# Self attention stage: copying the repeated high parts of the score stacks on the chip instead of loading them twice

## Chip, cores and metric

One NeuronCore of a Trainium2 chip runs the whole kernel. The metric is the device time of the program in microseconds (us). The profile is one execution of the same program, with times of instructions and transfers.

## What is computed

A gated block of two attentions over x, 32 batches of 100 rows and 512 columns, 16 heads of 32:

```
x = x + tanh(g_xattn) * cross_attention(layernorm(x), ctx_1024)
x = x + tanh(g_ffn)   * self_attention(layernorm(x))
```

The change touches the second line alone. There queries, keys and values come from one product, a similarity of each query with a guide vector sorts the 95 token rows of a batch into two classes, each class attends to its own class and to 5 register rows, and the register rows get the mean of what they would get with either class:

```
q, k, v = split(layernorm(x) @ W_qkv);  sim = mean over heads of cos(q, q_g), scaled to 0..1;  pos = sim > 0.9
logits  = (q * HD**-0.5) @ k^T                       # per batch and head, 100 x 100
x_pos, x_neg = softmax(logits | keys of pos) @ v, softmax(logits | keys of not pos) @ v
reg_out = (x_pos[:REG] + x_neg[:REG]) / 2;  tok_out = where(pos, x_pos, x_neg)
out     = concat(reg_out, tok_out) @ W_proj + b_proj
```

## The kernel before, in words

Four stages follow each other: `stage_queries`, `stage_cross`, `stage_rows` (projections of the second attention, written to DRAM as `qk_parts`, `values`, `x1` and the class `tables`) and `stage_self` (L1563), which is the last 340 us and the only one whose loops change.

**Split operands.** fp32 products are made from parts: a high part rounded to the fp32r type and the low rest. `qk_parts` holds four of them: q high, q low, k high, k low, each 512 x 3200. A score product is q_hi k_hi + q_lo k_hi + q_hi k_lo. The kernel gets it from one matmul per head by stacking along the contraction: `q_stack` has the 32 dims of q high in partitions 0 to 31, of q low in 32 to 63, of q high again in 64 to 95; `k_stack` has k high in 0 to 31, k high again in 32 to 63, k low in 64 to 95. Partitions 96 and 97 of both hold two class rows (the tables), which mask the keys. One stack holds a pair of batches (2 x 100 columns) for 16 heads. There are STACKS = 3 buffers of each, so pair n uses buffer n % 3. Pair 0 is loaded in `stage_rows`.

**Loads of a pair** (`load_pair` in the SyncE block; `load_stacks` L928, DMAs L932; `load_tables` L936, DMAs L941 and L943). Eight DMAs: q high and low together, q high again, k high again, k high and low together (two of 800 KB and two of 400 KB), and four small ones for the tables. All count on `pair_in[buf]`.

**Register copies** (`copy_registers` L947, done at L951 by GpSimd): the five register queries are put a second time into the q stack, for the second class. They read partitions 0 to 95, so they wait for the pair. For pair n they stand in batch 2n - 2.

**A batch.** Every engine's program is written out by hand as `body(b)`, six in a row for the buffers and a loop over them (`all_batches`); the bodies are software pipelined: body(b) scores batch b + 1, turns and mixes batch b, and projects batch b - 1. In body(b):

- TensorE: turn_probs(b, 0), score(b+1, 0), turn 1, score 1, turn 2, score 2, mix(b, 0) and (b, 1), half of project(b-1), turn 3, score 3, the other half, mix(b, 2) and (b, 3). Lines: turn L1834, score L1827, mix L1845, project L89 to L91.
- ScalarE: high_part(b-1) (L1705), then exponentials(b+1, 0 to 3), each four ACTIVATEs of one head (L1713).
- VectorE: turn_back(b, 0), shift_of(b+1, 0), fold_registers(b-1) (L1762, L1764), turn_back 1, split_mix(b-1) (L1768), shift 1, turn_back 2, shift 2, invert(b+1, 0), turn_back 3, shift 3, invert 1, result(b-1), invert 2, invert 3. Lines: turn_back L1750, shift_of L1739, invert L1746, result L1775. result(b-1) writes `y[odd]`, so it waits until the store of two batches before has left that buffer (`stored`).
- GpSimd: scale(b+1, j) (L1679) behind each invert, which frees turn_probs(b+1, j).
- SyncE's DMA queue, one for all of this stage's transfers, in order: store(b-1) (L1635, waits for result(b-1)), the x1 rows of batch b + 2 (L1619), the values of batch b + 3 (L1616, waits for the end of mix(b, 3)), and in an even body the eight loads of pair b/2 + 3 (wait for the last score of pair b/2). A DMA that waits holds all behind it.

So pair n + 3 is asked for in body(2n) and first needed by the register copies of body(2n + 4).

Of the kernel before, what the change touches and what calls it, by code (L numbers as in the profile page):

```python
# [23 lines left out]
ACT = mybir.ActivationFunctionType  # L24
# [45 lines left out]
def f32(ap):  # L70

    return ap.bitcast(F32)
# [814 lines left out]
STACKS = 3  # L887
# [6 lines left out]

QUERIES_AT = S
TW = QUERIES_AT + S + 2 * SIDE
A_PAIR_LOADS = 8


PLACED = 2  # L900
# [24 lines left out]
        self.cleared, self.copies_done = m.sem("cleared"), m.sem("copies_done")  # L925


def load_stacks(engine, qk_parts, q_stack, k_stack, first, landed):  # L928
# [634 lines left out]
def stage_self(nc, shared, begin, qk_parts, values_dram, x1_dram, table_dram, out):  # L1563
    with ExitStack() as ctx:
# [26 lines left out]
        proj_full, y_ready = m.sem("proj_full"), m.sem("y_ready")  # L1591
        stored = [m.sem(f"stored{i}") for i in range(2)]
        cleared = m.sem("cleared")

        block = ctx.enter_context(nc.Block())

        def all_batches(engine, body):


            for i in range(RING):  # L1600
                body(i, i, i // DEEP, i // 2, i, False)
            with engine.Fori(1, TAIL // RING) as u:
                for i in range(RING):
                    body(u * RING + i, i, u * (RING // DEEP) + i // DEEP, u * STACKS + i // 2, RING, False)
            for b in range(TAIL, B):
                body(b, b % RING, b // DEEP, b // 2, RING, b == B - 1)

        @block.sync
        def _(sp):
            def load_pair(first, buf):  # L1610

                load_stacks(sp, qk_parts, q_stack[buf], k_stack[buf], first, pair_in[buf])
# [10 lines left out]
            load_pair(2, 1)  # L1623
            load_values(1, 1)
            load_x1(0, 0)
            load_x1(1, 1)
            for n in range(2, DEEP):
                load_values(n, n)
                load_x1(n, n)
            for n in range(2, STACKS):  # L1630
                load_pair(2 * n, n)
# [24 lines left out]
            for b in range(TAIL, B):  # L1656
                body(b, b % RING, b // DEEP, b // 2, RING, b == B - 1, b + DEEP - 1 < B, b + DEEP < B, b + RING < B)
            store(B - 1, 1)
            for odd in range(2):
                sp.wait_ge(stored[odd], 16 * B // 2)  # L1660

        @block.gpsimd
        def _(pool):
            gaps = [(buf, at) for buf in range(1, STACKS) for at in (REG, 2 * QR - 1)]
            for n, (buf, at) in enumerate(gaps):
                if n:
                    pool.wait_ge(cleared, n)
# [3 lines left out]
            def copies(buf, pairs_before):  # L1671
                pool.wait_ge(pair_in[buf], (pairs_before + 1) * 16 * A_PAIR_LOADS)
                copy_registers(pool, q_stack[buf], unit_column, copies_done)

            def scale(b, odd, j):

                pool.wait_ge(inv_done, b * HPT + j + 1)
                quarter = prob[:, j, :, :]
                pool.tensor_tensor(quarter, quarter,  # L1679
                                   repeated(inv[odd][:, j * KT:(j + 1) * KT].unsqueeze(2), 2, S), ALU.mult  # L1680
                                   ).then_inc(scaled, 1)

            for b in range(RING):
                for j in range(HPT):
                    scale(b, b % 2, j)
                if b % 2 == 0:
                    copies((b + 2) // 2 % STACKS, (b + 2) // RING)
            with pool.Fori(1, TAIL // RING) as u:
                for i in range(RING):
                    for j in range(HPT):  # L1690
                        scale(u * RING + i, i % 2, j)
                    if i % 2 == 0:
                        copies((i + 2) // 2 % STACKS, u + (i + 2) // RING)
            for b in range(TAIL, B):
                for j in range(HPT):
                    scale(b, b % 2, j)
                if b % 2 == 0 and b + 2 < B:
                    copies((b + 2) // 2 % STACKS, (b + 2) // RING)

        @block.scalar  # L1700
        def _(act):
# [15 lines left out]
            def body(b, i, deep, pair, before, last):  # L1717
                odd = i % 2
                if before:
                    high_part(b - 1, 1 - odd)  # L1720
                if not last:
# [12 lines left out]
        def _(dve):  # L1734
# [43 lines left out]
            def body(b, i, deep, pair, before, last):  # L1778
                odd = i % 2
                turn_back(b, 0)  # L1780
                if not last:
                    shift_of(b + 1, 0)
# [33 lines left out]

        @block.tensor
        def _(pe):
            def score(b, i, j, pairs_before):

                buf, odd = i // 2, i % 2
                if not odd and j == 0:
                    pe.wait_ge(pair_in[buf], (pairs_before + 1) * 16 * A_PAIR_LOADS)
# [36 lines left out]
            def body(b, i, deep, before, last, step):  # L1860
# [2 lines left out]
                    pe.wait_ge(pt_done, b * HPT - 1)  # L1863
                turn_probs(b, 0)
                if not last:
                    score(b + 1, at, 0, step + (i + 1) // RING)
                if before:
                    pe.wait_ge(pt_done, b * HPT)
                turn_probs(b, 1)
# [20 lines left out]
                mix(b, odd, 3, place, deep)  # L1890

            for j in range(HPT):
                score(0, 0, j, 0)
# [56 lines left out]
```

## Time and profile before

| | us |
|---|---|
| device time, median of 3 runs | 2592.28 |
| lowest and highest | 2587.09, 2594.41 |
| the profiled execution: its own device time | 2588.93 |
| the profiled execution: span of the profile | 2587.1 |
| busy in the span: TensorE matmul, VectorE, ScalarE, GpSimd | 2478.7, 1804.8, 1332.2, 491.6 |

The page of the profile gives busy time for whole engines, the span in 40 slices of 64.7 us, and the costliest groups of instructions. The self stage is slices 35 to 40. A row of a timeline gives start, duration, engine, line, output <- input, and in brackets the idle time of the engine just before with what ended it.

### The profile page before, as it was taken

How to read it: one execution, taken by the hardware profiler on the slowest of the kernel's cores; microseconds unless marked ns; L12 is line 12 of the kernel's file. 1: busy time of each engine (PE TensorE's matmuls, PEld its weight loads, DVE VectorE, ACT ScalarE, POOL GpSimd, SP SyncE). 2: the span in 40 equal slices, each digit the busy share in tenths (PEclk: the TensorE clock that was granted, in tenths of full speed). 3: DMA queues.
4: the chain of work that ended last, by engine and by line, in shares of the span. 5: the costliest groups of instructions: out<-in, count | busy, mean ns of one | idle time of the engine just before them, and what ended most of it. 6: DMA issues, size and time to landing. Idle time of an engine off the chain costs nothing. (4 is left out here: it accounts for less than half of the span.)

```text
span 2587.1 us, 47522 instructions
## 1 busy us (share of the span) xinstructions
PE 2478.7 (96%) x17128; PEld 2223.4 (86%) x17128; DVE 1804.8 (70%) x2998; ACT 1332.2 (51%) x3000; POOL 491.6 (19%) x412
## 2 busy tenths in 40 slices
PE   6899999999999999999999999999959999889998
PEld 6889999999999999999999999999858888677776
DVE  7567777777777777777777777777757666565665
ACT  3355555555555545555555555545534444455564
POOL 0311111111111111111111111111024333133333
PEclk9999999999999999999999999999969999889999
DMA  7645554555545555545554455554459999899994
GB/s 223 205 122 131 124 131 120 131 128 131 132 117 128 130 133 128 131 117 130 129 132 122 128 125 129 131 132 126 106 150 192 214 211 198 207 175 189 192 185 105
DMA packets 324312, 379.82 MB, mean 147 GB/s; under 512 B 125814, under 2 KB 231702, under 8 KB 324118
## 3 DMA queue, kind: packets, MB, share of 16 engines
q1 hardware_dynamic: 322414, 375.71, 61.2%
q8 instruction: 132, 2.16, 0.4%
q10 hardware_dynamic: 1704, 1.43, 0.2%
q14 instruction: 62, 0.51, 0.1%
HBM read 162.48 MB, written 72.57 MB: 91 GB/s over the span
## 5 line engine op out<-in xcount | busy, mean ns | idle before, releaser
L740 DVE TENSOR_TENSOR c_parted<-c_prob,c_parted 128x600 fp32r<-128x600 f32 x512 | 400.6, 783 | 363.4 <-ACT c_prob L686 363.4
L864 PE MATMUL c_mix<-c_parted,c_v 120*66 120x200 f32 (+1 forms) x3072 | 544.9, 270 | 0.7 <-DVE c_parted L740 0.6
L849 PEld LDWEIGHTS c_pair<-c_q_stack,c_k_stack 100*120 100x120 f32 (+1 forms) x3072 | 517.7, 186 | 10.7 <-issue 6.1
L849 PE MATMUL c_pair<-c_q_stack,c_k_stack 100*120 100x100 f32 (+1 forms) x3072 | 520.0, 227 | 6.1 <-DVE c_parted L740 4.5
L726 DVE TENSOR_REDUCE c_peak<-c_pair 100x1 f32<-100x724 f32 x512 | 456.9, 908 | 55.2 <-PE c_pair L811 39.7
L682 ACT ACTIVATE c_parted<-c_pair 128x600 fp32r<-128x600 f32 x512 | 344.9, 674 | 283.0 <-PE c_pair L849 282.8
L864 PEld LDWEIGHTS c_mix<-c_parted,c_v 120*66 120x66 f32 (+1 forms) x3072 | 418.3, 140 | 3.1 <-DVE c_parted L740 0.9
L664 ACT ACTIVATE c_v<-c_work 120x512 fp32r<-120x512 f32 (+1 forms) x192 | 115.7, 603 | 442.3 <-PE c_work L91 442.3
L686 ACT ACTIVATE c_prob<-c_pair 128x600 f32<-128x600 f32 x512 | 341.4, 667 | 0.0
L811 PE MATMUL c_pair<-c_k_stack,c_q_stack 96*100 96x362 f32 x1024 | 254.4, 329 | 0.0
L617 POOL TENSOR_TENSOR c_ct_lo<-e_stage,c_ct_hi 128x722 fp32r<-128x722 f32 x64 | 111.8, 1747 | 747.1 <-ACT c_ct_hi L650 747.1
L617 POOL TENSOR_TENSOR f_ct_lo<-e_stage,f_ct_hi 128x722 fp32r<-128x722 f32 x60 | 104.8, 1747 | 718.5 <-ACT f_ct_hi L650 718.5
L811 PEld LDWEIGHTS c_pair<-c_k_stack,c_q_stack 96*100 96x100 f32 x1024 | 169.6, 166 | 60.4
L674 ACT ACTIVATE c_k_hi<-c_work,f_key_bias 128x362 fp32r<-128x362 f32 (+1 forms) x256 | 144.9, 567 | 105.3 <-PE c_work L91 85.7
L720 DVE SCALAR_TENSOR_TENSOR c_k_lo<-c_work,f_key_bias,c_k_hi 128x362 fp32r<-128x362 f32 (+1 forms) x256 | 149.8, 586 | 54.4 <-ACT c_k_hi L674 54.4
L1713 ACT ACTIVATE s_prob<-s_scores,s_shift 106x100 f32<-106x100 f32 x512 | 168.1, 368 | 34.5 <-DVE s_shift L1739 34.5
L89 PE MATMUL c_work<-f_ct_hi,w_wk_hi 128*128 128x362 f32 (+1 forms) x512 | 176.7, 345 | 8.6 <-PEq L153 4.5
L89 PE MATMUL c_work<-c_ct_hi,w_wk_hi 128*128 128x362 f32 (+1 forms) x512 | 175.0, 342 | 0.0
L91 PE MATMUL c_work<-f_ct_hi,w_wk_lo 128*128 128x362 f32 (+1 forms) x512 | 169.4, 331 | 0.0
L90 PE MATMUL c_work<-f_ct_lo,w_wk_hi 128*128 128x362 f32 (+1 forms) x512 | 169.1, 330 | 0.0
L91 PE MATMUL c_work<-c_ct_hi,w_wk_lo 128*128 128x362 f32 (+1 forms) x512 | 167.9, 328 | 0.0
L90 PE MATMUL c_work<-c_ct_lo,w_wk_hi 128*128 128x362 f32 (+1 forms) x512 | 167.9, 328 | 0.0
(205 smaller groups left out, 5292.7 us busy)
## 6 DMA issues: line engine op xcount, KB each, us to landing
c_k_stack<-c_k_hi SPq DMA_DIRECT2D x1024, 90.2 KB, 2.1
e_stage<-in_ctx SPq DMA_DIRECT2D x32, 1444.0 KB, 6.3
c_k_stack<-c_k_lo SPq DMA_DIRECT2D x512, 90.2 KB, 2.1
c_q_stack<-q_parts SPq DMA_DIRECT2D x192, 100.0 KB, 2.4
mix_parts<-w_mixed SPq DMA_DIRECT2D x64, 200.0 KB, 3.2
r_parts<-mix_parts SPq DMA_DIRECT2D x22, 512.0 KB, 7.1
s_q_stack<-qk_parts SPq DMA_DIRECT2D x10, 800.0 KB
s_k_stack<-qk_parts SPq DMA_DIRECT2D x10, 800.0 KB
```

Source lines behind the costliest of these rows:

```text
L89: pe.matmul(out, left_hi, right_hi, start=first, stop=False)
L90: pe.matmul(out, left_hi, right_lo, start=False, stop=False)
L91: return pe.matmul(out, left_lo, right_hi, start=False, stop=last)
L617: pool.tensor_tensor(ct_lo[odd][:, k, :], columns[:, k, :], ct_hi[odd][:, k, :], ALU.subtract).then_inc(ct_lo_done, 1)
L682: act.activation(parted[i % PR][:, :, 0, :].rearrange("p (a t) s -> p a t s", a=2), logits, ACT.Exp).then_inc(exp_hi_done, 1)
L686: act.activation(prob[i % 2][:, :, :].rearrange("p (a t) s -> p a t s", a=2), logits, ACT.Exp).then_inc(exp_done, 1)
L726: dve.tensor_reduce(peak[:, i:i + 1], pair[i % 2][0:S, :, 0:HALF], AX.XY, ALU.max).then_inc(peak_done, 1)
L740: dve.tensor_tensor(p[:, :, 1, :], prob[i % 2][:], p[:, :, 0, :], ALU.subtract).then_inc(p_lo_done, 1)
L811: last = pe.matmul(pair[i % 2][0:S, bank, 0:HALF], q_stack[0:STACK, i, :], k_stack[0:STACK, i, cols], start=True, stop=True)
L849: return pe.matmul(pair[i % 2][0:r, t // (CT // 2), col:col + S], k_stack[:, i, c_cols(t)], q_stack[:, i, :], start=True, stop=True)
L864: return pe.matmul(mix[g % 2][0:VW, at * 2 * S:(at + 1) * 2 * S], v[0:r, t, i, :], parted[i % PR][0:r, t, :, :].rearrange("p a s -> p (a s)"),
L1713: last = act.activation(prob[:, j, k, :], scores[0:QR, j, k * S:(k + 1) * S], ACT.Exp, bias=shift[:, at:at + 1], scale=-1.0, accum_out=tot ...
```

## The change

From pair 3 on `load_pair` issues only the first of each stack's two loads: q high and low into partitions 0 to 63, and k high and low into 32 to 95. The other third of each stack is copied on the chip in four pieces of four heads, 32 partitions by 4 x 200 columns: the q third by ScalarE (partitions 0 to 31 to 64 to 95), the k third by VectorE (partitions 32 to 63 to 0 to 31). Both do the pieces of pair b/2 + 2 in body(b): pieces 0 and 1 in the even body, 2 and 3 in the odd one, one after the first half of the exponentials (ScalarE) or ahead of turn_back 3 (VectorE), one at the end of the exponentials or ahead of result. Each piece waits for all of the pair's loads. GpSimd's register copies and the pair's first score now wait for the pieces too. Pairs 0 to 2 are loaded whole as before; the order of the two k loads is exchanged in all pairs. Bodies 2 to 27 hold the pieces of pairs 3 to 15.

```
+WHOLE_LOADS, PAIR_LOADS = 8, 6
+def pair_landed(buf, before):
+    return 16 * (PAIR_LOADS * (before + 1) + (WHOLE_LOADS - PAIR_LOADS if buf < WHOLE_PAIRS else 0))
...
-    for stack, at, places in ((q_stack, SIDE, ((0, 0, 2), (2, 0, 1))), (k_stack, 0, ((0, 2, 1), (1, 2, 2)))):
-        for place, part, parts in places:
+    for stack, at, places in ((q_stack, SIDE, ((0, 0, 2), (2, 0, 1))), (k_stack, 0, ((1, 2, 2), (0, 2, 1)))):
+        for place, part, parts in places if whole else places[:1]:
...
+        def thirds_in(i, before, more):
+            ahead = (i + 4 - i % 2) // 2
+            if not more or (before < RING and ahead < WHOLE_PAIRS):
+                return 0, 0, ()
+            return ahead % STACKS, ahead // STACKS, (2, 3) if i % 2 else (0, 1)
...
# GpSimd, ahead of copy_registers
+                if whole is not True:
+                    pool.wait_ge(q_third, HPT * (STACKS * pairs_before + buf - WHOLE_PAIRS + 1))
...
# ScalarE
+            def copy_third(buf, before, n):
+                act.wait_ge(pair_in[buf], pair_landed(buf, before))
+                heads = slice(n * HPT, (n + 1) * HPT)
+                act.activation(q_stack[buf][2 * HD:3 * HD, heads, SIDE:SIDE + 2 * S],
+                               f32(q_stack[buf][0:HD, heads, SIDE:SIDE + 2 * S]), ACT.Copy).then_inc(q_third, 1)
...
                 if not last:
-                    for j in range(HPT):
-                        exponentials(b + 1, 1 - odd, j)
+                    exponentials(b + 1, 1 - odd, 0)
+                    exponentials(b + 1, 1 - odd, 1)
+                for n in pieces[:half]:
+                    copy_third(buf, u + turns, n)
+                if not last:
+                    exponentials(b + 1, 1 - odd, 2)
+                    exponentials(b + 1, 1 - odd, 3)
+                for n in pieces[half:]:
+                    copy_third(buf, u + turns, n)
...
# VectorE
+            def copy_third(buf, before, n):
+                dve.wait_ge(pair_in[buf], pair_landed(buf, before))
+                heads = slice(n * HPT, (n + 1) * HPT)
+                dve.tensor_copy(k_stack[buf][0:HD, heads, 0:2 * S], f32(k_stack[buf][HD:2 * HD, heads, 0:2 * S])
+                                ).then_inc(k_third, 1)
...
                     invert(b + 1, 1 - odd, 0)
+                for n in pieces[:half]:
+                    copy_third(buf, u + turns, n)
                 turn_back(b, 3)
                 if not last:
                     shift_of(b + 1, 3)
                     invert(b + 1, 1 - odd, 1)
+                for n in pieces[half:]:
+                    copy_third(buf, u + turns, n)
...
# TensorE, ahead of the first score of a pair
+                    if not whole:
+                        pe.wait_ge(q_third, HPT * (STACKS * pairs_before + buf - WHOLE_PAIRS + 1))
+                        pe.wait_ge(k_third, HPT * (STACKS * pairs_before + buf - WHOLE_PAIRS + 1))
```

## Rows read from the trace of the kernel before

**Rows 1.** The page: busy share of the 16 DMA engines in 40 slices.
```profile
DMA  7645554555545555545554455554459999899994
```

**Rows 2.** Starts of mix(b, 2) and (b, 3) on TensorE, b = 4, 28, 30.
```profile
2315.31 1.31 PE L1845 MATMUL s_out_bank<-s_pt,s_values 100*32 100x106 f32 x16
...
2551.43 1.31 PE L1845 MATMUL s_out_bank<-s_pt,s_values 100*32 100x106 f32 x16
...
2568.31 1.31 PE L1845 MATMUL s_out_bank<-s_pt,s_values 100*32 100x106 f32 x16
```

**Rows 3.** Waits, self stage (engine, line, releaser: us in total, times, longest).
```profile
DVE s_y L1775 <- DMA out<-s_y: 39.9, 13, 5.7
```

**Rows 4.** SyncE's queue, pair 7's loads in body 8 (start, duration).
```profile
2362.47 2.76 SPq L932 DMA_DIRECT2D s_q_stack<-qk_parts  x2
...
2378.03 1.23 SPq L943 DMA_DIRECT2D s_q_stack<-tables  x1
2379.35 0.67 SPq L1635 DMA_DIRECT2D out<-s_y  x1
```

**Rows 5.** DMA issues by line and size: the large load of a stack.
```profile
s_q_stack<-qk_parts SPq DMA_DIRECT2D x10, 800.0 KB
```

**Rows 6.** Stretches: us, busy (x count) of PE, PEld, DVE, ACT, POOL, PEclk, DMA share, GB/s.
```profile
2286.00:2298.00 12.00, 12.00 (x109) 9.87 (x108) 9.07 (x25) 8.99 (x51) 4.31 (x7) 1.00 1.12 203
2298.00:2302.00 4.00, 4.00 (x39) 3.18 (x37) 1.17 (x3) 2.68 (x16) 1.30 (x2) 1.00 0.37 91
...
2326.00:2338.00 12.00, 11.85 (x111) 9.89 (x109) 9.31 (x25) 8.02 (x45) 5.46 (x8) 1.00 1.13 182
...
2542.00:2562.00 20.00, 19.63 (x181) 16.02 (x180) 13.28 (x36) 13.02 (x74) 9.27 (x13) 1.00 0.34 114
```

**Rows 7.** Timeline of an undisturbed batch: body 10 and the start of body 11.
```profile
2365.22 0.57 PE L1834 MATMUL s_turned<-e_ident,s_prob 106*100 106x106 f32 x4
...
2369.74 0.17 DVE L1746 RECIPROCAL s_inv<-s_total 106x4 f32<-106x4 f32 x1
2370.76 0.60 DVE L1750 COPY s_pt<-s_turned 100x424 f32<-100x424 f32 x1 [0.85 <-PE s_turned L1834]
...
2372.72 0.75 DVE L1775 SCALAR_TENSOR_TENSOR s_y<-s_out_bank,p_gate,s_x 100x512 f32<-100x512 f32 x1 [0.79 <-PE s_out_bank L91]
...
2373.63 1.67 POOL L1679 TENSOR_TENSOR s_prob<-s_prob,s_inv 106x400 f32<-106x400 f32 x2 [0.78 <-DVE s_inv L1746]
...
2375.11 0.55 PE L1834 MATMUL s_turned<-e_ident,s_prob 106*100 106x106 f32 x4
```

**Rows 8.** Groups by form: mean ns of one stands after the busy us.
```profile
L726 DVE TENSOR_REDUCE c_peak<-c_pair 100x1 f32<-100x724 f32 x512 | 456.9, 908 | 55.2 <-PE c_pair L811 39.7
...
L1440 DVE COPY w_mixed<-w_mixed 32x224 f32<-32x224 f32 x1 | 0.3, 265 | 0.0
...
L650 ACT ACTIVATE c_ct_hi<-e_stage 128x722 fp32r<-128x722 f32 x64 | 51.0, 796 | 0.0
```

**Rows 9.** Timeline near 2267 us: GpSimd beside a VectorE instruction with two inputs.
```profile
2267.07 0.59 POOL L951 TENSOR_TENSOR s_q_stack<-s_q_stack,p_unit_column 96x80 fp32r<-96x80 f32 x2 [8.18 <-DMA s_q_stack<-tables]
2267.63 3.29 POOL L1679 TENSOR_TENSOR s_prob<-s_prob,s_inv 106x400 f32<-106x400 f32 x4
2267.73 5.33 DVE L1806 TENSOR_TENSOR s_w_lo<-e_stage,s_w_hi 128x2048 fp32r<-128x2048 f32 x1 [1.62 <-ACT s_w_hi L1726]
```

**Rows 10.** A group by form: the same operation and shape in the stage before.
```profile
L1304 DVE TENSOR_TENSOR r_w_lo<-r_raw,r_w_hi 128x2048 fp32r<-128x2048 f32 x1 | 2.3, 2282 | 0.0
```

**Rows 11.** SyncE's queue: first loads of pairs 1 and 3, last table of pair 3.
```profile
2249.64 1.29 SPq L932 DMA_DIRECT2D s_q_stack<-qk_parts  x2
...
2284.54 3.01 SPq L932 DMA_DIRECT2D p_q_stack<-qk_parts  x2
...
2298.33 1.36 SPq L943 DMA_DIRECT2D p_q_stack<-tables  x1
```

**Rows 12.** VectorE's wait for a store in body 3.
```profile
2305.20 0.75 DVE L1775 SCALAR_TENSOR_TENSOR s_y<-s_out_bank,p_gate,s_x 100x512 f32<-100x512 f32 x1 [5.69 <-DMA out<-s_y]
```

More of the change, by code:

```diff
@@ L925, in __init__, with load_stacks @@
         self.cleared, self.copies_done = m.sem("cleared"), m.sem("copies_done")
-def load_stacks(engine, qk_parts, q_stack, k_stack, first, landed):
-    for stack, at, places in ((q_stack, SIDE, ((0, 0, 2), (2, 0, 1))), (k_stack, 0, ((0, 2, 1), (1, 2, 2)))):
-        for place, part, parts in places:
+def load_stacks(engine, qk_parts, q_stack, k_stack, first, landed, whole=True):
+    for stack, at, places in ((q_stack, SIDE, ((0, 0, 2), (2, 0, 1))), (k_stack, 0, ((1, 2, 2), (0, 2, 1)))):
+        for place, part, parts in places if whole else places[:1]:
             src = qk_parts[part:part + parts].rearrange("a (d h) n -> (a d) h n", h=H)
@@ L1600, in all_batches, with load_pair @@
             for i in range(RING):
-                body(i, i, i // DEEP, i // 2, i, False)
+                body(i, i, i // DEEP, i // 2, i, False, 0)
             with engine.Fori(1, TAIL // RING) as u:
                 for i in range(RING):
-                    body(u * RING + i, i, u * (RING // DEEP) + i // DEEP, u * STACKS + i // 2, RING, False)
+                    body(u * RING + i, i, u * (RING // DEEP) + i // DEEP, u * STACKS + i // 2, RING, False, u)
             for b in range(TAIL, B):
-                body(b, b % RING, b // DEEP, b // 2, RING, b == B - 1)
+                body(b, b % RING, b // DEEP, b // 2, RING, b == B - 1, b // RING, (b + 4 - b % 2) // 2 < PAIRS)
+        def thirds_in(i, before, more):
[3 more added lines that the diff above has]
+            return ahead % STACKS, ahead // STACKS, (2, 3) if i % 2 else (0, 1)
         @block.sync
         def _(sp):
-            def load_pair(first, buf):
-                load_stacks(sp, qk_parts, q_stack[buf], k_stack[buf], first, pair_in[buf])
+            def load_pair(first, buf, whole=False):
+                load_stacks(sp, qk_parts, q_stack[buf], k_stack[buf], first, pair_in[buf], whole)
                 load_tables(sp, table_dram, q_stack[buf], k_stack[buf], first, pair_in[buf])
@@ L1622, in _ @@
             sp.wait_ge(cleared, 2 * (STACKS - 1))
-            load_pair(2, 1)
+            load_pair(2, 1, True)
             load_values(1, 1)
@@ L1630, in _ @@
             for n in range(2, STACKS):
-                load_pair(2 * n, n)
+                load_pair(2 * n, n, True)
             def store(b, odd):
@@ L1669, in _, with copies @@
             pool.wait_ge(cleared, 2 * (STACKS - 1))
-            def copies(buf, pairs_before):
-                pool.wait_ge(pair_in[buf], (pairs_before + 1) * 16 * A_PAIR_LOADS)
+            def copies(buf, pairs_before, whole=False):
+                pool.wait_ge(pair_in[buf], pair_landed(buf, pairs_before))
+                if whole is not True:
+                    pool.wait_ge(q_third, HPT * (STACKS * pairs_before + buf - WHOLE_PAIRS + 1))
                 copy_registers(pool, q_stack[buf], unit_column, copies_done)
@@ L1686, in _ @@
                 if b % 2 == 0:
-                    copies((b + 2) // 2 % STACKS, (b + 2) // RING)
+                    copies((b + 2) // 2 % STACKS, (b + 2) // RING, (b + 2) // 2 < WHOLE_PAIRS)
             with pool.Fori(1, TAIL // RING) as u:
@@ L1697, in _ @@
                 if b % 2 == 0 and b + 2 < B:
-                    copies((b + 2) // 2 % STACKS, (b + 2) // RING)
+                    copies((b + 2) // 2 % STACKS, (b + 2) // RING, (b + 2) // 2 < WHOLE_PAIRS)
         @block.scalar
@@ L1715, in exponentials, with body @@
                 last.then_inc(exp_done, 1)
-            def body(b, i, deep, pair, before, last):
+            def copy_third(buf, before, n):
[3 more added lines that the diff above has]
+                               f32(q_stack[buf][0:HD, heads, SIDE:SIDE + 2 * S]), ACT.Copy).then_inc(q_third, 1)
+            def body(b, i, deep, pair, before, last, u, more=True):
                 odd = i % 2
@@ L1720, in body @@
                     high_part(b - 1, 1 - odd)
+                buf, turns, pieces = thirds_in(i, before, more)
+                half = len(pieces) // 2
                 if not last:
-                    for j in range(HPT):
-                        exponentials(b + 1, 1 - odd, j)
+                    exponentials(b + 1, 1 - odd, 0)
[7 more added lines that the diff above has]
+                    copy_third(buf, u + turns, n)
                 if not before:
@@ L1776, in result, with body @@
                                          ).then_inc(y_ready, 1)
-            def body(b, i, deep, pair, before, last):
+            def copy_third(buf, before, n):
[3 more added lines that the diff above has]
+                                ).then_inc(k_third, 1)
+            def body(b, i, deep, pair, before, last, u, more=True):
                 odd = i % 2
+                buf, turns, pieces = thirds_in(i, before, more)
+                half = len(pieces) // 2
                 turn_back(b, 0)
@@ L1818, in _, with score @@
         def _(pe):
-            def score(b, i, j, pairs_before):
+            def score(b, i, j, pairs_before, whole=False):
                 buf, odd = i // 2, i % 2
                 if not odd and j == 0:
-                    pe.wait_ge(pair_in[buf], (pairs_before + 1) * 16 * A_PAIR_LOADS)
+                    pe.wait_ge(pair_in[buf], pair_landed(buf, pairs_before))
                     pe.wait_ge(copies_done, 2 * STACKS * pairs_before + 2 * buf + 2)
+                    if not whole:
+                        pe.wait_ge(q_third, HPT * (STACKS * pairs_before + buf - WHOLE_PAIRS + 1))
+                        pe.wait_ge(k_third, HPT * (STACKS * pairs_before + buf - WHOLE_PAIRS + 1))
                 for k in range(KT):
@@ L1865, in body @@
                 if not last:
-                    score(b + 1, at, 0, step + (i + 1) // RING)
+                    score(b + 1, at, 0, step + (i + 1) // RING, before < RING and (i + 1) // 2 < WHOLE_PAIRS)
                 if before:
@@ L1892, in _ @@
             for j in range(HPT):
-                score(0, 0, j, 0)
+                score(0, 0, j, 0, True)
             for i in range(RING):
```

3 lines of the change are left out of this document (2 added, 1 removed).

## The prediction

> **What bounds the kernel now.** I read the page first. The last six slices, the self stage, show DMA busy at eight or nine tenths, where the long cross stage shows four or five [rows 1]. A share says little alone, so I then took the pace. The start of mix(b, 2), (b, 3) marks each batch: from b = 4 to 28 it takes 2551.43 - 2315.31 = 236.1 us, 9.84 us a batch or **19.68 a pair**; from b = 28 to 30, with no pair left to load, (2568.31 - 2551.43) / 2 = 8.44 a batch or **16.88 a pair** [rows 2]. TensorE is busy 19.63 of 20 us there, at clock 1.00, with DMA at 0.34 [rows 6]. So 2.8 us in each pair is not computation. The list of waits says what it is: result waits 39.9 us in 13 times for `out`, the store two batches before [rows 3]. The store is small, but SyncE's queue shows what it stands behind: pair 7's loads take from 2362.47 to 2379.26 to issue, and only then the next store goes [rows 4]. Issuing is slow since the DMA engines are full: 1.12 and 1.13 busy while the stacks are loaded [rows 6]. The chain is: bytes, queue, store, result, the inverts behind result on VectorE, GpSimd's scale, TensorE's turn. The self stage is bound by its transfers.
>
> **What the change removes.** A pair has 2 x (800 + 400) KB of stack loads [rows 5], 1200 KB of values, x1 and out, and some 50 KB of tables: 3.65 MB. Two of 400 KB go: 2.85 MB. At the present pace bytes alone would allow 19.68 x 2.85 / 3.65 = 15.4 us a pair, below the 16.88 of computation. So the bytes stop being the bound, and the most that 12 pairs, from b = 4 to 28, can give is 12 x 2.80 = 33.6 us.
>
> Stretches of the trace show that the engines are not evenly loaded: 1.12 while stacks are loaded, 0.37 in the 4 us behind pair 3's loads [rows 6]. The Trainium skill (DMA: Bandwidth & Descriptors, Why a DMA increments its semaphore by 16 and not by 1) says that a transfer uses as many engines, up to 16, as divide its slowest dimension: 16 for the stacks, 10 for rows of 100, 2 for the tables. By that rule, my estimate is that the busiest engine goes from 296 to 246 KB a pair, and the bound by transfers would be 16.4 instead of 15.4 us. Both are below 16.88, so the sum is the same.
>
> **What it adds on VectorE.** One copy of 32 x 800 in each place. The nearest rows: a COPY of 224 elements takes 265 ns, a reduction of 724 takes 908 ns [rows 8]. In proportion these give 0.95 and 1.00 us; if half of the small copy's time were a fixed part, 0.13 + 0.47 = 0.60. I take 0.65, since the copy is the same operation and a part of so short a time will be fixed; ends 0.55 and 1.0. The gaps: after invert 0 VectorE is idle 0.85 us until turn_back 3, and 0.79 before result [rows 7]. At 0.65 both copies fit into them; at 1.0 each pushes by 0.2. Behind result stand invert 2 and 3; scale 2 starts at 2373.63, lasts 0.84, and its turn starts at 2375.11 [rows 7], so 0.6 us is spare. Cost: nothing, cover 0.6 us.
>
> **What it adds on ScalarE.** An ACTIVATE of 722 elements between SBUF tiles takes 796 ns [rows 8], so 0.88 us for 800, twice a batch. The first delays exponentials 2 and 3 by about 0.7. Exponential 2 was done near 2371.7, its invert stands behind result until 2373.4, and invert 3 would slip from 2373.5 to 2373.9, whose turn comes 4 us later. The second stands in ScalarE's wait for the fold. Cost: nothing.
>
> GpSimd's register copies and the first score wait for pieces made a body or more before: nothing.
>
> **The new wait.** This is the term that decides. Pair n + 3 was needed in body(2n + 4); its first pieces now stand in body(2n + 2), a pair earlier, and VectorE and ScalarE stand still until all of it has landed. Count from the first turn of an even body: in body 10 that is 2365.22, invert 0 ends at 2369.91, so the piece is due at +4.7; result ends at +8.25 [rows 7]. Store, x1 and values go then, and the loads follow 1.5 us later. About 1.0 us of lateness is absorbed (the 0.6 us above, and the gaps that the copies leave).
>
> How long do loads take to land? Pair 3's started at 2284.54 on quiet engines, its last table went at 2299.69 [rows 11]; the engines were full from 2286 to 2298, then at 0.37 [rows 6]. That is 1.5 to start, 12.3 for the stacks, about 3 for the tail. For two thirds of the stacks: 1.5 + 8.2 + 3 = 12.7. In steady state 600 KB of store, x1 and values stand directly ahead; at 203 GB/s [rows 6] they add 3. From the store's issue at +8.3 that is 15.7 minus the overlap of the start, **15 to 15.7**, so landing at +23.3 to +24.0. The next piece is due one pair later at P + 4.7 + 1.0. So P = 17.6 to 18.3: the loop through the landing, not the computation, sets the pace. Bounds: pair 1, issued at 2249.64 and landed at 2267.07 [rows 9, 11], took 17.4 for a whole pair with other loads beside it; two thirds are 11.6, which gives P = 16.88 (computation bounds). If nothing were gained over its 17.4, P = 17.4 + 9.8 - 5.7 = 21.5. I take **P = 18.0**: 12 x (19.68 - 18.0) = 20.2 us gained.
>
> **The start.** Pair 3's loads are issued at 2284.54 as before, since SyncE is still busy with whole pairs 1 and 2. Its pieces stand in body 2, which begins at about 2284.4, so they are due at 2289.1; it lands at 2284.5 + 12.7 = 2297.2. Wait 8.1, of which 1.0 is absorbed, and about 1 us comes back as TensorE's lower clock behind the stall: 8 us. In exchange, the wait of 5.69 us for store 0 in body 3 [rows 12], which cost 6.9 with its clock, is gone, since the store's queue is shorter. Net loss 1.2 us.
>
> **Sum.** The profiled execution took 2588.9 us (span 2587.1). 2588.9 - 20.2 + 1.2 = **2570 us**, 0.7% less. The profiled execution lies 3.4 us under the median of 2592.3, a difference that the range covers.
>
> **Rivals.**
> *Full gain.* The loads land in 12 to 13 us, P = 16.9: 2588.9 - 33.6 + 1.2 = 2556. For it: two thirds of pair 1's time. Against: store, x1 and values right ahead of each load. Chance 0.2.
> *VectorE's copies collide with GpSimd.* The trace shows VectorE's L1806 taking 5.33 us while four scales ran beside its first 3.19 [rows 9], where the same operation took 2.28 [rows 10]: it stood until GpSimd was done. If a copy behaves so, one behind invert 0 meets the scale which that invert frees. If VectorE comes first, a scale with 1.5 us or more to spare is late, and nothing is lost. If GpSimd does, both copies wait 0.85 us, and result is late by about 1.2, of which 0.6 is lost. On top of P = 18.0 half of it shows: 24 batches x 0.3 = 7, so 2577. Chance 0.15.
> The Trainium skill (SBUF — State Buffer, SBUF: two separate sides) states that the two engines share a port pair as an exclusive lock, taken by VectorE instructions in a two-port mode or with two SBUF inputs; the trace agrees for the two-input kind with the 5.33 us, and no row before shows a copy beside GpSimd.
> *The expected gain is eaten.* Landing takes 17 us from the store's issue, P = 19.6: 2588.9 + 1.2 - 1 = 2589, within 0.3%. Chance 0.13.
> *Slower: the earlier deadline.* The pieces' deadline is a pair earlier, so three stacks work as two: the next loads go only behind a result which stands behind the pieces, and the engines run dry in each loop. It decides from P = 19.8, a landing 17.2 us after the store's issue. At the upper bound P = 21.5: 2588.9 + 1.2 + 12 x 1.8 = 2612. For it: 0.37 busy behind pair 3, a slow tail that does not shrink with the bytes [rows 6]. Against: no third of the bytes has ever been without weight on full engines. Chance 0.1.
>
> **Numbers.** Forecast 0.42; full gain 0.2; collision 0.15; eaten 0.13; slower 0.1. The predicted time is the forecast's. The range goes from the full gain, 2556, up to 2588, which leaves out the slower case and most of the eaten one. About 0.3% (8 us) is what a measurement of this kernel can tell from none. Faster by more: 0.77; within: 0.13; slower: 0.1.
>
> **What would show it.** Result's wait for `out` falls from 39.9 us to under 5. New waits for `tables` appear before the copies in VectorE and ScalarE: 8 us in body 2, 0 to 2 us in each even body. Mix marks stand 17.3 to 18.8 us a pair from b = 4 to 28. 26 bodies x 2 copies of about 0.65 us on VectorE and 0.88 on ScalarE. DMA moves 10.6 MB less. Wrong if the marks stay at 19.7, or if copies wait for GpSimd each time.

## The result, and the profile after

The changed kernel takes **2584.3 us** in the median of 16 runs (2579.96 to 2586.95), the kernel before 2592.22 us in 16 runs beside them (2585.11 to 2596.53). The ratio is 0.9972, with a 95% interval of 0.9965 to 0.9979: faster by 0.28%, or 7.9 us, where 20 had been forecast. The profiled execution took 2583.70 us (span 2581.9, against 2587.1 before).

First the marks that gave the pace before, mix(b, 2), (b, 3) for b = 4, 28 and 30, from the timeline of TensorE after (start, duration; mix is L1891 here):

```profile
2324.49 1.31 PE L1891 MATMUL s_out_bank<-s_pt,s_values 100*32 100x106 f32 x16
...
2546.15 1.31 PE L1891 MATMUL s_out_bank<-s_pt,s_values 100*32 100x106 f32 x16
...
2563.03 1.31 PE L1891 MATMUL s_out_bank<-s_pt,s_values 100*32 100x106 f32 x16
```

From b = 4 to 28 it takes 221.66 us, **18.47 a pair**, where before it took 19.68 [rows 2]: 14.5 us gained. But the mark of b = 4 stands at 2324.49 instead of 2315.31. The self stage itself begins 1.0 us earlier in this execution, which its first products show, mix(2, 0) and (2, 1) before and after:

```profile
2286.64 1.31 PE L1845 MATMUL s_out_bank<-s_pt,s_values 100*32 100x106 f32 x16
...
2285.64 1.31 PE L1891 MATMUL s_out_bank<-s_pt,s_values 100*32 100x106 f32 x16
```

So **the start loses 10.2 us** (9.2 by the marks and 1.0 from the earlier begin). -14.5 + 10.2 - 1.0 = -5.3, and the spans differ by -5.2: the difference lies in these two places.

The page's DMA line shows the self stage, the last six slices, at six to eight tenths and two in the last, where it was at eight or nine and four in the last [rows 1]; the bytes went from 379.82 to 369.16 MB:

```profile
DMA  7645545555545555545555455554458999876762
DMA packets 310584, 369.16 MB, mean 143 GB/s; under 512 B 125398, under 2 KB 217974, under 8 KB 310390
```

The waits after (us in total, times, longest). Result's wait for `out`, 39.9 us before [rows 3], has gone. In its place both copying engines wait for tables:

```profile
DVE p_k_stack L1812 <- DMA p_q_stack<-tables: 23.0, 5, 13.2
ACT p_q_stack L1736 <- DMA p_q_stack<-tables: 20.8, 5, 12.7
DVE s_k_stack L1812 <- DMA s_q_stack<-tables: 16.5, 7, 2.6
```

The groups by form (busy us, mean ns of one behind the bar) give what an added copy costs, 565 ns on VectorE and 874 on ScalarE. GpSimd's scale went from 854 to 973 in the mean:

```profile
L1812 DVE CAST s_k_stack<-s_k_stack 32x800 fp32r<-32x800 f32 x32 | 18.1, 565 | 17.3 <-DMA s_q_stack<-tables 16.5
...
L1736 ACT ACTIVATE s_q_stack<-s_q_stack 32x800 fp32r<-32x800 f32 x32 | 28.0, 874 | 14.0 <-DMA s_q_stack<-tables 13.4
...
L1695 POOL TENSOR_TENSOR s_prob<-s_prob,s_inv 106x400 f32<-106x400 f32 x128 | 123.2, 973 | 168.3 <-DVE s_inv L1777 168.3
```

**A loop.** The chain of waits over one pair in the steady part, followed back from the end and printed in order of time (start, duration, what), shows what sets the pace:

```profile
2341.35 0.06 DVE s_k_stack L1812
...
2341.85 0.56 DVE s_pt L1781
2342.42 0.48 DVE s_shift L1770
2342.93 0.18 DVE s_inv L1777
2343.14 0.56 DVE s_k_stack L1812
2343.74 0.76 DVE s_y L1806
...
2344.69 0.32 SPq L1649
...
2346.36 0.62 SPq L938
...
2348.51 1.96 SPq L947
...
2352.61 7.30 DMA p_q_stack<-tables
2359.93 0.06 DVE p_k_stack L1812
```

Read it as a circle. VectorE's first piece starts when a pair has landed (2341.35). Turn_back 3, shift 3, invert 1 and the second piece follow, then result; only then does the store go (2344.69), behind it x1, values, the stacks and the four tables, the last at 2352.61. It lands 7.30 us later, and at 2359.93 the first piece of the next pair starts. One round is 2359.93 - 2341.35 = 18.58 us: the pace. TensorE itself loses only 18.47 - 16.88 = 1.6 us in it, and GpSimd and ScalarE are no link of this chain. Part of what was gained over the old pace is clock: in the same stretch of 220 us TensorE's granted clock was 0.93 in the mean before and is 1.00 after, where its stops are shorter.

```profile
2320.00:2540.00 220.00, 201.84 (x1679) 164.69 (x1678) 133.45 (x356) 129.69 (x736) 80.30 (x110) 0.93 0.94 189
...
2320.00:2540.00 220.00, 210.71 (x1809) 170.08 (x1808) 172.89 (x428) 181.03 (x839) 100.66 (x118) 1.00 0.65 151
```

Stretches of the round above (us, busy of PE, PEld, DVE, ACT, POOL, clock, DMA share, GB/s) show that the transfers are not the bound as such, for they run dry in each round:

```profile
2344.00:2348.00 4.00, 3.33 (x36) 2.85 (x35) 3.47 (x11) 3.35 (x15) 2.09 (x3) 1.00 0.42 117
2348.00:2356.00 8.00, 8.00 (x74) 6.68 (x75) 6.98 (x19) 7.25 (x34) 4.69 (x6) 1.00 1.07 223
2356.00:2360.00 4.00, 4.00 (x25) 2.74 (x22) 1.56 (x5) 2.01 (x13) 0.85 (x1) 1.00 0.52 161
2360.00:2363.00 3.00, 2.67 (x25) 2.14 (x24) 2.91 (x7) 2.98 (x15) 1.23 (x1) 1.00 0.04 16
```

**The start.** In body 2 pair 3 is late. The rows are its first load and last table in SyncE's queue, VectorE's first piece, and the mix that TensorE could then go on with:

```profile
2285.59 0.69 SPq L938 DMA_DIRECT2D p_q_stack<-qk_parts  x1
...
2295.09 0.98 SPq L949 DMA_DIRECT2D p_q_stack<-tables  x1
...
2301.25 0.57 DVE L1812 CAST p_k_stack<-p_k_stack 32x800 fp32r<-32x800 f32 x1 [13.18 <-DMA p_q_stack<-tables]
...
2302.38 1.62 PE L1891 MATMUL s_out_bank<-s_pt,s_values 100*32 100x106 f32 x8 [10.86 <-DVE s_pt L1781]
```

VectorE stands 13.18 us, TensorE 10.86. The stretches behind it show what this costs in clock:

```profile
2302.00:2308.00 6.00, 5.62 (x32) 5.31 (x32) 5.38 (x15) 5.26 (x26) 2.90 (x3) 0.50 0.34 95
2308.00:2314.00 6.00, 6.00 (x30) 4.66 (x30) 1.68 (x5) 3.86 (x19) 1.23 (x1) 0.50 1.08 190
```

TensorE is busy 11.62 us there at a granted clock of 0.50, its lower level of 1.2 GHz, and does what takes 5.8 us at 1.00.

### The profile page after: what moved, and what is told of

Read it like the earlier page. It is cut to its first block and busy times, and to the rows that moved or that the text cites. A ratio compares the mean times of both kernels' runs of the same rounds, so it can differ in the third digit from the quotient of the medians.

```text
span 2581.9 us, 47629 instructions
## 1 busy us (share of the span) xinstructions
PE 2476.8 (96%) x17128; PEld 2220.1 (86%) x17128; DVE 1834.8 (71%) x3050; ACT 1377.5 (53%) x3052; POOL 508.7 (20%) x412
## 2 busy tenths in 40 slices
DMA packets 310584, 369.16 MB, mean 143 GB/s; under 512 B 125398, under 2 KB 217974, under 8 KB 310390
## 5 line engine op out<-in xcount | busy, mean ns | idle before, releaser
L849 PEld LDWEIGHTS c_pair<-c_q_stack,c_k_stack 100*120 100x120 f32 (+1 forms) x3072 | 518.4, 186 | 10.1 <-issue 5.5
L1729 ACT ACTIVATE s_prob<-s_scores,s_shift 106x100 f32<-106x100 f32 x512 | 168.2, 360 | 13.9 <-DVE s_shift L1770 13.2
```

Source lines behind the costliest of these rows:

```text
L849: return pe.matmul(pair[i % 2][0:r, t // (CT // 2), col:col + S], k_stack[:, i, c_cols(t)], q_stack[:, i, :], start=True, stop=True)
L1729: last = act.activation(prob[:, j, k, :], scores[0:QR, j, k * S:(k + 1) * S], ACT.Exp, bias=shift[:, at:at + 1], scale=-1.0, accum_out=tot ...
```

## The experiments

Each text on record names its theories. The main ones that stood after the result were these. **L**, the loop: the pace is the time from the store's issue to the landing plus VectorE's way from the first piece to the store. **B**, the bytes: the transfers are still the bound. **W**, the work: the copies, or their meeting GpSimd, cost it. For the start, **S**: pair 3 comes too late for its earlier due time. All ratios are against the kernel before on the same chip, and "pace" is the distance of the marks from b = 4 to 28 in the profile, over 12. Each was run 4 times, the second and the fifth 10 times. The diffs are against the changed kernel.

### Copies and their waits left out

```
 def copy_third(buf, before, n):
+    return
     ...wait_ge(pair_in[buf], pair_landed(buf, before))
```

(on both engines, with the waits of GpSimd and TensorE for the pieces)

> The changed kernel with the pieces, their waits for the loads and the waits for the pieces left out; the two loads stay away, so the thirds of pairs 3 to 15 hold old data. Theory L (a loop sets the pace: the loads land 15.3 us after the store's issue, and 3.3 us pass from the landing through VectorE's piece and result to the next store; the start loses 12 us in body 2): both waits are gone, the pace from b = 4 to 28 goes from 18.5 to 16.9 us a pair, the stall of 13.2 us in body 2 goes, 2553 to 2560 us. Theory B (transfers still bound): the bytes are the same, the pace stays at 18.4 to 18.5. Theory W (the copies' own work on VectorE, ScalarE and beside GpSimd sets the pace): 16.9 as well, so this run tells B from the other two.

Measured: 2555.45 us, ratio 0.9857 (0.9837 to 0.9877), pace 202.51 / 12 = **16.88**. That is to 0.01 us the computation's floor [rows 2], with the same bytes as after. Theory B fell: 2.85 MB a pair do not hold the pace. L and W both stood.

### The pieces of even bodies at the body's end

```
-                half = len(pieces) // 2
+                half = len(pieces) // 2 if odd else 0
...
# VectorE, even bodies: ahead of result -> behind invert 3
+                for n in () if odd else pieces:
+                    copy_third(buf, u + turns, n)
```

> The changed kernel with the two pieces of each even body put behind the last invert (VectorE) and the last exponentials (ScalarE); the same instructions, bytes and waits. Theory L: result no longer stands behind the wait and the pieces are due 3.8 us later, so the loop is open and the pace is 16.9 to 17.2; the stall in body 2 shrinks from 13 to about 9 us; 2562 to 2568 us. Theory W: the work is all there, the pace stays near 18.5, 2580 to 2585 us. Theory B: stays near 18.5.

Measured: 2591.51 us, ratio 1.0004 (0.9994 to 1.0013), pace 19.45. A miss for theory L, which had this faster than the change, and for W and B too, which had a pace near 18.5. The waits for tables were gone but for body 2 (10.1 us), so the loop was open. But here the pieces follow invert 2 and 3, which free GpSimd's scales. The timeline at the end of body 8:

```profile
2361.21 2.00 POOL L1695 TENSOR_TENSOR s_prob<-s_prob,s_inv 106x400 f32<-106x400 f32 x2 [0.58 <-DVE s_inv L1777]
...
2361.30 2.33 DVE L1812 CAST p_k_stack<-p_k_stack 32x800 fp32r<-32x800 f32 x2
...
2363.56 0.58 DVE L1781 COPY s_pt<-s_turned 100x424 f32<-100x424 f32 x1
...
2364.27 0.56 PE L1882 MATMUL s_turned<-e_ident,s_prob 106*100 106x106 f32 x4 [1.22 <-DVE s_pt L1781]
```

Two copies take 2.33 us instead of 1.13, as VectorE and GpSimd are in each other's way; turn_back of the next body comes late, and TensorE waits for it. The 1.2 us more are the 1.22 that TensorE waits. The rest of the pace is clock: from 2330 to 2550 us TensorE is idle for 14.75 us, 1.3 a pair, and its granted clock is 0.94 in the mean, where loads first (the next run) has 1.00, which is some 1.1 us a pair more (0.06 of 205.25 busy us, over 11.3 pairs). Moving the copies out of one loop put them at the head of VectorE's next body, where there was no slack. So the collision that the prediction had as a rival exists, but only where a copy meets a scale that began first.

### The pair's loads ahead of store, x1 and values

```
                 odd = i % 2
+                if odd == 0 and more_pairs:
+                    sp.wait_ge(scored, (b + 2) * HPT)
+                    load_pair(b + RING, i // 2)
                 if before:
                     store(b - 1, 1 - odd)
```

(and gone from the end of the body)

> The changed kernel with SyncE's order in an even body changed: the pair's loads stand ahead of store, x1 and values instead of behind them. Theory L: the loads leave at about +6 us of a body instead of +9.8 and have no 600 KB in front, they land before they are due, the pace is 16.9 to 17.2 and the start keeps its stall; 2563 to 2569 us. Theory W: pace stays near 18.5. Theory B: stays near 18.5.

Measured: 2563.49 us, ratio 0.9894 (0.9878 to 0.9911), pace 16.91. The marks of b = 4 and 28 in its timeline:

```profile
2324.05 1.31 PE L1890 MATMUL s_out_bank<-s_pt,s_values 100*32 100x106 f32 x16
...
2526.97 1.31 PE L1890 MATMUL s_out_bank<-s_pt,s_values 100*32 100x106 f32 x16
```

This settles the pace. All copies, waits and bytes are those of the change; only the loads no longer stand behind result in SyncE's queue. The loop is cut, and the pace is the floor. The start stays in the main: VectorE waits 11.3 us in body 2, where it waited 13.2. The run is 28 us faster than the kernel before.

### Everything loaded whole, pieces and waits kept

```
-WHOLE_LOADS, PAIR_LOADS = 8, 6
+WHOLE_LOADS, PAIR_LOADS = 8, 8
-        for place, part, parts in places if whole else places[:1]:
+        for place, part, parts in places:
```

> The changed kernel with all eight loads for every pair, and the pieces and their waits kept (they write once more what was loaded). It is the new wait without the saving. Theory L: the loads land some 4.2 us later (800 KB at 190 GB/s), so the pace is 15.3 + 4.2 + 3.3 = 22.8 us a pair, about 52 us over the changed kernel: 2630 to 2645 us. Theory B: the pace is the old one, 19.7, 2595 to 2603 us. Theory W: 19.7 as well, the old bound.

Measured: 2648.63 us, ratio 1.0223 (1.0206 to 1.024), pace 23.58. This is the loop with the 800 KB a pair back in it: 5.1 us more in each round. L is the theory that it fits, but the pace is 0.8 and the time 4 us above what that text had. Its waits:

```profile
DVE s_k_stack L1812 <- DMA s_q_stack<-tables: 43.3, 8, 8.2
```

So the change consists of two opposite effects. The earlier due time together with the copies (1.1 us of it, as the run with waits alone shows below) would have cost 3.9 us a pair (23.58 - 19.68), and the smaller loads give 5.1 back; 1.2 are left.

### Pair 3 whole as well

```
-WHOLE_PAIRS = 3
+WHOLE_PAIRS = 4
-                    load_pair(b + RING, i // 2)
+                    load_pair(b + RING, i // 2, before == 0 and i == 0)
```

> The changed kernel with pair 3 loaded whole too (WHOLE_PAIRS = 4), so that the first pieces stand in body 4; SyncE's order as in the changed kernel. Theory S (the 13.2 us that VectorE stands in body 2 are nearly all lost, since pair 3 cannot land before its pieces are due): that wait goes, in exchange the store's wait in body 3 comes back in part (before: 5.7 us); mix mark of b = 4 comes 7 to 10 us earlier, 2573 to 2578 us, with the pace unchanged at 18.5. Rival (the stall only moves one pair on: pair 4's loads leave as late as pair 3's): the first wait is 10 us or more in body 4 and the time stays at 2582 to 2586.

Measured: 2587.59 us, ratio 0.9983 (0.9973 to 0.9992). The stall of body 2 was gone and stood in body 4 instead, with the old wait for a store ahead of it:

```profile
2307.20 0.75 DVE L1807 SCALAR_TENSOR_TENSOR s_y<-s_out_bank,p_gate,s_x 100x512 f32<-100x512 f32 x1 [6.69 <-DMA out<-s_y]
...
2323.14 0.56 DVE L1813 CAST s_k_stack<-s_k_stack 32x800 fp32r<-32x800 f32 x1 [11.07 <-DMA s_q_stack<-tables]
```

The copies need each pair a pair earlier, and with this order of the queue the price is paid once, wherever the first piece stands. The rival of that text named the wait (10 us or more in body 4), though the time came 1.6 us above its range; theory S, with a stall of pair 3 alone, fell.

### Waits kept, copies left out

```
                 ...wait_ge(pair_in[buf], pair_landed(buf, before))
+                return
                 heads = slice(n * HPT, (n + 1) * HPT)
```

(both engines; GpSimd and TensorE do not wait for pieces)

> The changed kernel with the copies of the pieces left out but their waits for the loads kept, and no waits for the pieces; the thirds of pairs 3 to 15 hold old data. Theory L: the loop stays closed, only the two pieces of 0.57 us between landing and result are missing from it, so the pace is 18.5 less 0.6 to 1.1, 17.4 to 17.9 us a pair, and the stall in body 2 stays; 2568 to 2576 us. Theory W (the work): with no work the pace is 16.9, 2562 us or less.

Measured: 2569.96 us, ratio 0.9908 (0.9891 to 0.9925), pace 17.37. SyncE's queue shows a round without copies: from one store of an odd batch to the next 2361.09 - 2343.87 = 17.22 us.

```profile
2343.87 0.32 SPq L1649 DMA_DIRECT2D out<-s_y  x1
...
2361.09 0.31 SPq L1649 DMA_DIRECT2D out<-s_y  x1
```

Two copies of 0.565 us are 1.13, and 18.47 - 17.37 = 1.10. So the copies cost their bare length, for they lie inside the loop, and the waits alone cost 0.49 a pair over the floor.

### Four table loads left out

```
-                load_tables(sp, table_dram, q_stack[buf], k_stack[buf], first, pair_in[buf])
+                if whole:
+                    load_tables(sp, table_dram, q_stack[buf], k_stack[buf], first, pair_in[buf])
```

> The changed kernel without the four small table loads of pairs 3 to 15 (rows 96 and 97 keep the tables of earlier pairs, so the classes are wrong). It asks what the landing's tail is, some 6 us from the last issue to the landing in the changed kernel's trace. Theory T1 (the tail is the small loads themselves, each held up behind full queues): landing comes 3 us or more earlier, the loop opens, pace 16.9 to 17.2, time 2562 to 2566 us. Theory T2 (the tail is the bulk, the small loads only sit at its end): landing 1 us earlier or less, pace 17.6 to 18.4, 2572 to 2582 us.

Measured: 2562.74 us, ratio 0.9884 (0.9867 to 0.99), pace 16.91. T1 was right: loads of 53 KB a pair (0.69 MB in all) set the landing back far enough to make 18.47 of 16.91. Behind body 2 only one copy still waits for a load, for 0.6 us, so how much earlier the landing comes can't be read here.

### Loads first, and pair 3 whole

The edits of the third and the fifth run together.

> Both repairs: the pair's loads ahead of store, x1 and values, and pair 3 loaded whole. Theories L and S add up: pace 16.9 to 17.2, no stall in body 2, 2552 to 2558 us, 1.3 to 1.5% under the kernel before and within 4 us of the run without pieces (2555.5). Rival: without the stall pair 4 lands late at its first pieces, and 3 us or more of the gain are lost again, 2559 to 2564 us.

Measured: 2562.02 us, ratio 0.9882 (0.9865 to 0.9898), pace 16.91. Its 1.5 us against loads first alone are inside both intervals. Again the rival was right; the stall took a third form: in body 3 TensorE waits for values, which now stand behind pair 3's whole loads.

```profile
2304.90 2.30 PE L1891 MATMUL s_out_bank<-s_pt,s_values 100*32 100x106 f32 x16 [9.66 <-DMA s_values<-values]
```

### Tables ahead of the stacks

```
+                load_tables(sp, table_dram, q_stack[buf], k_stack[buf], first, pair_in[buf])
                 load_stacks(sp, qk_parts, q_stack[buf], k_stack[buf], first, pair_in[buf], whole)
-                load_tables(sp, table_dram, q_stack[buf], k_stack[buf], first, pair_in[buf])
```

> The changed kernel with the four table loads ahead of the stacks' loads instead of behind them, for every pair; same bytes. It asks why the small loads cost so much. Theory Q (they come late only because they stand behind full queues): in front they are gone by the time the stacks are through, landing comes some 3 us earlier, pace 16.9 to 17.2, 2562 to 2568 us. Theory E (they are slow work on the few engines that carry them, wherever they stand): the engines that carry them reach the end of the stacks' part as late as before, pace 18.2 to 18.6, 2581 to 2586 us.

Measured: 2565.41 us, ratio 0.9894 (0.9878 to 0.9911), pace 206.5 / 12 = 17.21. SyncE's queue and VectorE's piece:

```profile
2341.67 0.32 SPq L1649 DMA_DIRECT2D out<-s_y  x1
...
2343.34 0.25 SPq L947 DMA_DIRECT2D p_k_stack<-tables  x1
...
2345.90 0.59 SPq L938 DMA_DIRECT2D p_k_stack<-qk_parts  x1
```

```profile
2355.61 0.57 DVE L1812 CAST p_k_stack<-p_k_stack 32x800 fp32r<-32x800 f32 x1 [1.14 <-DMA p_k_stack<-qk_parts]
```

The pace and the time are those of Q, and E fell; of the 3 us that Q had for the landing 1.3 came. Nothing differs from the change but two lines exchanged. A table load takes 0.25 us to issue where it took 0.62 to 1.96 in the round shown before, and the pair has landed 13.9 us after its store's issue (2355.61 - 2341.67) instead of 15.2. With VectorE's 3.3 that makes 17.2, the pace measured. So the loop's formula holds for a second value of the landing. The start gained as well: VectorE waits 7.6 us in body 2 instead of 13.2, TensorE 5.4 instead of 10.9, and from mix(1, 2) to mix(4, 2) it takes 36.3 us instead of 42.4 (before the change 32.2). So this order gives 15 us by the pace and 6 by the start.

### Both orders together, without and with pair 3 whole

Tables first, and loads first from body 2 on; then the same with pair 3 whole.

> Two changes of order, no byte less: tables ahead of the stacks, and from body 2 on the pair's loads ahead of store, x1 and values (body 0 keeps the old order, so that values 3 are not behind pair 3). The pace is 16.9 in any case. The start decides: by theory Q pair 3 lands 2 to 4 us earlier, 2558 to 2561 us; by theory E nothing is gained over the run with the loads first, 2562 to 2565 us.

> The same with pair 3 loaded whole as well. No pieces stand in bodies 2 and 3 and values 3 keep their place, so the wait of 9.7 us for values that ended the run with both repairs is gone; the store's wait in body 3 should show instead (6.7 us in the run with four whole pairs), less if the tables leave sooner. 2555 to 2560 us; if the wait of one resource is always replaced by one of the next, since the first 7 MB take their time whoever waits for them, 2560 to 2564 us.

Measured: 2562.2 us, ratio 0.9877 (0.9858 to 0.9896), pace 16.91, with one wait of 8.9 us in body 2; and 2560.91 us, ratio 0.9879 (0.9862 to 0.9896), with waits of 7.7 us in body 4, 2.4 for a store and 0.9 for values. These do not differ from loads first by what was measured, and both lie in the forecasts of the rivals in the two texts, not in those of the theories. The five versions with a changed order that keep the computation end 1.1 to 1.2% under the kernel before, and by the ratios 5 to 10 us above the run without copies. Most of that rest is the start: from mix(1, 2) to mix(4, 2) the changed kernel takes 42.4 us, loads first 39.9, loads first with pair 3 whole 37.9, both orders together 36.7, and the run without copies 30.6. The orders took a part of it away, none took all.

## Why the prediction was right and wrong

**Right: what bounded the kernel before, and the first terms.** The wait for `out` went, 10.66 MB fewer were moved (forecast 10.6), new waits for tables appeared before the copies of both engines, and the copies took 0.565 and 0.874 us (forecast 0.65 and 0.88). The landing was forecast 15 to 15.7 us after the store's issue, and in the round shown it is 2359.93 - 2344.69 = 15.24. The mechanism of the forecast, a loop through the landing that sets a pace above the computation's, was the one that the runs showed.

**Wrong: "about 1.0 us of lateness is absorbed", 5.7 us of the sum.** The 1.0 us was slack that TensorE has against VectorE: 0.6 us before a turn, and gaps that the copies leave. Such slack counts for work that hangs off the path. Here VectorE itself is in the loop: from the landing to the store's issue it runs the first piece, turn_back 3, shift 3, invert 1, the second piece and result, 2363.24 - 2359.93 = 3.31 us, and only then can the next loads be asked for, however long TensorE would have waited. The undisturbed distance from due time to store was 3.55 us, of which the prediction took off 1.0 and should have taken off 0.24. 15.24 + 3.31 = 18.55, measured 18.47, forecast 18.0: 12 x 0.47 = 5.7 us less gain. (The 0.76 alone would be 9.1; that the landing came at the low end of its forecast, and the mean round a little shorter than the one shown, gave 3.4 back.) For the same reason "Cost: nothing" for the copies on VectorE was wrong. The argument looked only at what a turn could spare, but each round was longer by both copies, as the run with waits alone shows: 1.10 of 1.13 us a pair.

**Wrong: the start, net loss 10.2 us instead of 1.2.** This is the larger part, and has two terms. First the landing of pair 3, "two thirds of the stacks: 1.5 + 8.2 + 3 = 12.7". It took 2301.25 - 2285.59 = 15.7, and was issued 1.05 us later than before while the stage began 1.0 earlier. 8.1 + 3.0 + 2.05 = 13.15, and VectorE's wait was 13.18. Scaling with the bytes was the failure: from the issue of the last table to the landing it took 6.2 us (2301.25 - 2295.09), a tail that did not shrink. And the engines were not quiet: in the stretch from 2280 to 2285.6 they were busy at 0.71 behind pair 2's loads, where before it was 0.48 (2280 to 2284.5). Second, "about 1 us comes back as TensorE's lower clock". The stall of the kernel before may have suggested that, 5.69 us [rows 12] which with its clock cost 6.9. But the 5.69 are VectorE's wait. TensorE itself stood 4.25 us there, so that its clock had cost some 2.6:

```profile
2307.11 0.92 PE L1834 MATMUL s_turned<-e_ident,s_prob 106*100 106x106 f32 x4 [4.25 <-POOL s_prob L1679]
```

In the changed kernel TensorE stood 10.86 us and then ran at 0.50 for 11.62 busy us, 5.8 us lost. 10.86 + 5.8 - 6.9 = 9.8, near the 10.2 found. Against the forecast 8.1 - 1.0 + 1.0 - 6.9 the wait was 5.1 us longer and the clock cost 4.8 more, while TensorE took up 2.3 us of the wait instead of 1.0.

Together 2570 + 5.7 + 9.0 = 2584.7, less 1.0 for the stage that began earlier: 2583.7, the time of the profiled execution.

**The rivals.** Full gain did not come, but the run with loads first reached its pace of 16.9 and 2563.5 us. The collision: in the change VectorE's copy starts first, at 2361.73, and a scale behind it takes 1.23 us instead of 0.85. The forecast's harmless case had such a scale with time to spare. Here, where the round is late anyway, it has none, and a turn waits 0.25 us for it; the pace does not come from there, since the copies cost no more than their length.

```profile
2361.73 0.56 DVE L1812 CAST p_k_stack<-p_k_stack 32x800 fp32r<-32x800 f32 x1
...
2361.77 1.23 POOL L1695 TENSOR_TENSOR s_prob<-s_prob,s_inv 106x400 f32<-106x400 f32 x1 [3.35 <-DVE s_inv L1777]
...
2363.06 0.57 PE L1880 MATMUL s_turned<-e_ident,s_prob 106*100 106x106 f32 x4 [0.25 <-POOL s_prob L1695]
```

The harmful case was shown where the copies were moved behind the last inverts. The slower rival named the mechanism, the earlier due time, which together with the copies costs 3.9 us a pair when bytes are not cut; its price at the present bytes was too high, its place was right.

**Open.** Why small loads behind full queues are slow to issue and land 7.3 us later was not taken apart: the runs show that their place in the queue costs it, not which engines they use. Nor was a form found that spares the start whole; a smaller first pair or other buffers were not tried. And no run has the new order without the copies, on the kernel before: there too a store stands behind a pair's loads, so what the order alone would give, and what the copies are worth beside it, is not known.

## What to carry to other kernels

When a change makes a consumer wait for a transfer earlier, draw the circle: from the landing through the consumer's own instructions to the point that issues the next transfer, and back. Its length is the pace; work inside it costs its full time, and slack seen by other engines buys nothing. Look in the issuing queue first: exchanging the order of DMAs that are there already gave 20 us more here, more than twice what the copies had given (the order was tried only with the copies in place). Where one consumer waits for large and small loads together, try the small ones first.

## What the runs showed of the hardware

**Small loads behind large ones.** In the steady rounds shown, a table load took 0.25 us to issue ahead of the stacks and 0.62 to 1.96 behind them, and landing came 7.30 us after the last issue with the 16 DMA engines busy at 0.52 in the mean of its last 4 us. The Trainium skill (DMA: Bandwidth & Descriptors, Why a DMA increments its semaphore by 16 and not by 1) says that a load with a slowest dimension of 2 goes to two engines only. The lower share in the tail would fit, but no row here shows single engines.

**The copy between partitions.** VectorE's 32 x 800 copy with rounding took 565 ns, less than the reduction of 724 elements at 908 [rows 8]: two thirds of its time, so the estimate in proportion (1.00 us) was far off.

**The shared port goes to who comes first.** A scale that began 0.04 us behind a copy took 1.23 us; two copies that began 0.09 us behind a scale took 2.33 together. The Trainium skill (SBUF — State Buffer, SBUF: two separate sides) has this as an exclusive lock, which whichever starts first holds for its whole instruction, for VectorE instructions in a two-port mode or with two SBUF inputs. Both rows agree in who has to wait, here for a copy with one input; the scale lost 0.38 us of the 0.52 that the copy still ran.

**The long product when it comes first.** L1849, the same operation as the one of 5.33 us [rows 9], took 2.29 us in the changed kernel. It began at 2266.57, and GpSimd's two register copies began 0.67 us behind it. This time they were the ones to wait, 2.07 us for what had taken 0.59 [rows 9]:

```profile
L1849 DVE TENSOR_TENSOR s_w_lo<-e_stage,s_w_hi 128x2048 fp32r<-128x2048 f32 x1 | 2.3, 2292 | 1.6 <-ACT s_w_hi L1757 1.6
...
2267.24 2.07 POOL L957 TENSOR_TENSOR s_q_stack<-s_q_stack,p_unit_column 96x80 fp32r<-96x80 f32 x2 [9.51 <-DMA s_q_stack<-tables]
```
